# Splitting the experts' weights one expert ahead of the tiles that use them

## The reference, cut to what matters

```python
scores = x @ router_DE                       # 4096 rows, 8 experts
topv, topi = top_k(scores, 2)
gates = sigmoid(masked scores)               # 0 for experts not chosen
routed_in = x[None] * gates[:, :, None]
mid = einsum('ead,edf->eaf', routed_in, w_in_eDF)      # D 256 -> F 512
sw  = einsum('ead,edf->eaf', routed_in, w_swiglu_eDF)
h = silu(mid) * sw
out = sum over e of einsum('eaf,efd->ead', h, w_out_eFD)
```

## Time and profile before

| | |
|---|---|
| median of 3 runs | 1818.01 us (1816.95 to 1818.47) |
| profiled execution, its own time | 1816.74 us |
| its span | 1814.9 us |
| PE busy | 1610.9 us, 89% |
| DVE busy | 946.8 us, 52% |
| ACT busy | 958.7 us, 53% |
| POOL busy | 449.5 us, 25% |
| mean granted clock of PE | 0.945 |

### The profile page before, as it was taken

One profiled execution on the slowest core, in us unless ns is written; L12 is line 12 of the kernel. 1 busy time (PEld: TensorE's weight loads), 2 busy tenths in 40 slices (PEclk: granted clock), 3 DMA queues, 4 the chain that ended last, 5 costly groups with the idle time before them and its releaser, 6 DMA issues. The chain is left out here.

```text
span 1814.9 us, 30860 instructions
## 1 busy us (share of the span) xinstructions
PE 1610.9 (89%) x10249; PEld 1109.6 (61%) x10250; DVE 946.8 (52%) x1826; ACT 958.7 (53%) x1528; POOL 449.5 (25%) x496
## 2 busy tenths in 40 slices
PE   7859999999999948998569999999579976997998
PEld 5633333333333327887458888888468976896887
DVE  6523543635445447777743333333376555756784
ACT  5449999999999924444422222222133434333332
POOL 0001111111121112555522222222144003001664
PEclk9969999999999968999889999999789988998999
DMA  8982415514523047211411111111302010000001
GB/s 272 265 260 39 67 36 88 89 33 70 95 47 55 18 134 261 88 60 46 142 53 52 49 49 52 52 46 52 107 24 94 1 59 0 1 1 4 24 27 44
DMA packets 79455, 134.18 MB, mean 74 GB/s; under 512 B 11600, under 2 KB 45904, under 8 KB 76208
## 3 DMA queue, kind: packets, MB, share of 16 engines
q1 hardware_dynamic: 72360, 111.86, 23.9%
q0 software_dynamic: 6992, 20.95, 3.6%
HBM read 74.63 MB, written 58.14 MB: 73 GB/s over the span
## 5 line engine op out<-in xcount | busy, mean ns | idle before, releaser
L713 ACT ACTIVATE probs<-ps_s 128x1024 f32<-128x1024 f32 (+3 forms) x640 | 511.9, 941 | 10.5 <-PE ps_s L763 7.0
L780 PE MATMUL ps_o<-probs,V 128*17 128x512 f32 (+3 forms) x2560 | 292.6, 536 | 0.3 <-POOL probs L701 0.3
L701 POOL TENSOR_SCALAR_AFFINE_SELECT probs<-probs 128x512 f32<-128x512 f32 x128 | 83.3, 653 | 440.4 <-ACT probs L713 438.5
L1445 DVE COPY slot_hT<-ps_hT 128x512 f32<-128x512 f32 x71 | 49.1, 691 | 193.5 <-PE ps_hT L1488 193.5
L763 PEld LDWEIGHTS ps_s<-Q_even,K_even 50*128 50x128 f32 x640 | 55.7, 186 | 137.3 <-ACT probs L713 119.9
L1498 PE MATMUL ps_slot_y<-we_out,slot_hT 128*128 x568 | 134.6, 380 | 1.4 <-DVE slot_hT L1445 0.9
L763 PE MATMUL ps_s<-Q_even,K_even 50*128 50x512 f32 (+3 forms) x640 | 124.7, 445 | 12.0 <-DMA Q_even<-shift_parts 11.3
L1978 POOL TENSOR_TENSOR h_lo<-h,h_hi 128x512 fp32r<-128x512 f32 x64 | 89.5, 1416 | 182.4 <-DVE h L2024 182.4
L763 PEld LDWEIGHTS ps_s<-Q_odd,K_odd 50*128 50x128 f32 x640 | 55.1, 183 | 123.8 <-ACT probs L713 116.4
L763 PE MATMUL ps_s<-Q_odd,K_odd 50*128 50x512 f32 (+3 forms) x640 | 123.1, 439 | 0.4
L1403 POOL DMA_INDIRECT routed_rows<-slot_y,home_row x71 | 69.4, 977 | 178.5 <-ACT slot_y L1422 173.8
(11 more groups left out here) (280 smaller groups left out, 3969.9 us busy)
## 6 DMA issues: line engine op xcount, KB each, us to landing
qk_stacks<-qk_hi SPq DMA_DIRECT2D x64, 256.0 KB, 3.9
slot_rows<-slots_in SPq DMA_DIRECT2D x71, 128.5 KB, 2.0
qk_stacks<-qk_lo SPq DMA_DIRECT2D x32, 256.0 KB, 4.0
Q_odd<-qk_stacks SPq DMA_DIRECT2D x8, 768.0 KB
K_odd<-qk_stacks SPq DMA_DIRECT2D x8, 768.0 KB
Q_even<-qk_stacks SPq DMA_DIRECT2D x6, 768.0 KB
K_even<-qk_stacks SPq DMA_DIRECT2D x6, 768.0 KB
X<-x SPq DMA_DIRECT2D x8, 512.0 KB, 4.4
```

The source lines that it names most:

```text
L701: pool.affine_select(out=block_of, in_=block_of, compare_op=ALU.is_ge, fill=0.0, base=0, pattern=[[0, HG], [1, P]], channel_multiplier=-1) ...
L713: act.activation(probs[:, at % PROB_BUFS, 2 * p:2 * p + 2, off:BT], ps_s[:, s % SCORE_BUFS, :, off:BT], ACT.Exp).then_inc(exp_ok, 1)
L780: last = pe.matmul(ps_o[32 * h:32 * h + DH + 1, s % 2, off:BT], k["V"][:, group, SEQ_TILES * b + t, h, :], probs[:, at % PROB_BUFS, h, off ...
L1445: dve.tensor_copy(hT[:, :, :], ps_h[:, :, :]).then_inc(hT_ok, 1)
```

## The change: each expert's weights split during the tile before its first possible use

ACT, DVE and POOL split expert 0 ahead of the first tile, and expert i+1 at or near the end of their body i, for i from 0 to 6: ACT makes both high parts, DVE the low part of `we_in`, POOL that of `we_swiglu`. Each expert is given at least one tile, so that tile i never needs an expert beyond i. PE waits in tiles 0 to 7 for the low parts of expert i: before the first expansion for `in_low`, before the gated one for `gate_low` (in tile 0 both count in `in_low`). The third matrices are loaded in two halves of four, with the loads of the rows of tiles 2 and 3 between the halves and those of 4 and 5 behind. The first eight bodies are written out (`head=4`) in place of two.

```diff
-def over_blocks(eng, count, body):
+def over_blocks(eng, count, body, head=1):
     pairs = count // 2
-    for j in range(2):
-        body(j, j, 0)
-    if pairs > 2:
-        with eng.Fori(1, pairs - 1) as n:
+    for i in range(2 * head):
+        body(i, i % 2, i // 2)
+    if pairs > head + 1:
+        with eng.Fori(head, pairs - 1) as n:
...
-                    link(dve.tensor_scalar(padded[:, :], count[:, :], float(P - 1), None, ALU.add))
+                    link(dve.tensor_scalar(padded[:, :], count[:, :], float(P - 1), float(P), ALU.add, ALU.max))
...
-        w_in = sem(k, "experts_w_in")
+        outs_in = sems(k, "experts_out_in", "first_half second_half")
...
-        w_high, w_low, home_ok = sems(k, "experts", "w_high w_low home_ok")
-        halves = [(hi[:, e], lo[:, e]) for e in range(EXPERTS) for hi, lo in ((wi_hi, wi_lo), (wg_hi, wg_lo))]
-        def low_weights(eng, own):
-            for n, (hi, lo) in enumerate(halves):
-                if (n % 3 == 2) == own:
-                    eng.wait_ge(w_high, n + 1)
-                    eng.tensor_tensor(lo, lo.bitcast(F32), hi.bitcast(F32), ALU.subtract).then_inc(w_low, 1)
+        w_high, in_low, gate_low, home_ok = sems(k, "experts", "w_high in_low gate_low home_ok")
+        HALF_EXPERTS = EXPERTS // 2
+        def high_weights(act, e):
+            for hi, lo in ((wi_hi, wi_lo), (wg_hi, wg_lo)):
+                act.activation(hi[:, e], lo[:, e].bitcast(F32), ACT.Copy).then_inc(w_high, 1)
+        def low_weight(eng, hi, lo, e, m, done):
+            eng.wait_ge(w_high, 2 * e + m + 1)
+            eng.tensor_tensor(lo[:, e], lo[:, e].bitcast(F32), hi[:, e].bitcast(F32), ALU.subtract).then_inc(done, 1)
+        def splits_next(i):
+            return isinstance(i, int) and i + 1 < EXPERTS
...
 # SP
                 load(0, 0)
                 load(1, 1)
-                for e in range(EXPERTS):
-                    sp.dma_start(wo[:, e], ...).then_inc(w_in, 16)
-                with sp.Fori(0, SLOT_TILES // 2 - 1) as n:
+                for half in range(2):
+                    for e in range(HALF_EXPERTS * half, HALF_EXPERTS * (half + 1)):
+                        sp.dma_start(wo[:, e], ...).then_inc(outs_in[half], 16)
+                    for i in (2 * half + 2, 2 * half + 3):
+                        sp.wait_ge(home_ok, i - 1)
+                        sp.wait_ge(x_ok, i - 1)
+                        load(i, i % 2)
+                with sp.Fori(2, SLOT_TILES // 2 - 1) as n:
...
 # POOL, body i
-                low_weights(pool, True)
                 clear(pool, k["stale"])
...
                     if not is_last(i, SLOT_TILES):
                         find_home(i + 1, 1 - j, n + j)
+                    if splits_next(i):
+                        low_weight(pool, wg_hi, wg_lo, i + 1, 1, gate_low)
                     hold(pool, k, home_ok, i + 1)
                     hold(pool, k, y_ok, i + 1)
...
 # ACT, body i
                     if not is_first(i):
                         result(i - 1, 1 - j, n - (1 - j))
+                    if splits_next(i):
+                        high_weights(act, i + 1)
...
 # DVE, body i
                         x_rest(i + 1, 1 - j)
+                    if splits_next(i):
+                        low_weight(dve, wi_hi, wi_lo, i + 1, 0, in_low)
...
 # PE, body i
+                    if isinstance(i, int) and i < EXPERTS:
+                        pe.wait_ge(in_low, i + 2 if i else 1)
                     expand(i, j, e, ps_m, wi_hi, wi_lo, mid_ok)
                     if not is_first(i):
                         turn_h(i - 1, 1 - j)
+                    if is_first(i):
+                        pe.wait_ge(in_low, 2)
+                    elif isinstance(i, int) and i < EXPERTS:
+                        pe.wait_ge(gate_low, i)
                     expand(i, j, e, ps_g, wg_hi, wg_lo, gated_ok)
```

More of the change, by code:

```diff
@@ L1375, in _ @@
                 load(1, 1)
-                for e in range(EXPERTS):
-                    sp.dma_start(wo[:, e], io["w_out_e"][e].rearrange("(c p) f -> p c f", p=P)).then_inc(w_in, 16)
-                with sp.Fori(0, SLOT_TILES // 2 - 1) as n:
+                for half in range(2):
+                    for e in range(HALF_EXPERTS * half, HALF_EXPERTS * (half + 1)):
+                        sp.dma_start(wo[:, e], io["w_out_e"][e].rearrange("(c p) f -> p c f", p=P)
+                                     ).then_inc(outs_in[half], 16)
+                    for i in (2 * half + 2, 2 * half + 3):
[3 more added lines that the diff above has]
+                with sp.Fori(2, SLOT_TILES // 2 - 1) as n:
                     for j in range(2):
@@ L1406, in _ @@
                 find_home(0, 0, 0)
-                over_blocks(pool, SLOT_TILES, body)
+                over_blocks(pool, SLOT_TILES, body, HALF_EXPERTS)
                 for j in range(2):
@@ L1431, in body @@
                         result(i - 1, 1 - j, n - (1 - j))
+                    if splits_next(i):
+                        high_weights(act, i + 1)
                 act.wait_ge(k["experts_in"], 16 * 2 * EXPERTS)
-                for hi, lo in halves:
-                    act.activation(hi, lo.bitcast(F32), ACT.Copy).then_inc(w_high, 1)
+                high_weights(act, 0)
                 turned(0, 0)
-                over_blocks(act, SLOT_TILES, body)
+                over_blocks(act, SLOT_TILES, body, HALF_EXPERTS)
                 result(SLOT_TILES - 1, 0, SLOT_TILES // 2)
@@ L1458, in body @@
                         x_rest(i + 1, 1 - j)
-                low_weights(dve, False)
+                    if splits_next(i):
+                        low_weight(dve, wi_hi, wi_lo, i + 1, 0, in_low)
+                low_weight(dve, wi_hi, wi_lo, 0, 0, in_low)
+                low_weight(dve, wg_hi, wg_lo, 0, 1, in_low)
                 x_rest(0, 0)
-                over_blocks(dve, SLOT_TILES, body)
+                over_blocks(dve, SLOT_TILES, body, HALF_EXPERTS)
                 turned(SLOT_TILES - 1, 0)
@@ L1492, in contract @@
                     e = expert_of(i)
-                    if is_first(i):
-                        pe.wait_ge(w_in, 16 * EXPERTS)
+                    if isinstance(i, int) and i % HALF_EXPERTS == 0 and i < EXPERTS:
+                        pe.wait_ge(outs_in[i // HALF_EXPERTS], 16 * HALF_EXPERTS)
                     pe.wait_ge(hT_ok, i + 1)
@@ L1515, in _ @@
                 turn_x(0, 0, 0)
-                pe.wait_ge(w_low, len(halves))
-                over_blocks(pe, SLOT_TILES, body)
+                over_blocks(pe, SLOT_TILES, body, HALF_EXPERTS)
                 turn_h(SLOT_TILES - 1, 0)
```

## The result

The changed kernel takes 1832.68 us (median of 4 runs, 1830.9 to 1834.59), the kernel before 1817.48 beside it (4 runs, 1815.93 to 1818.47). The ratio is 1.0087, its 95% interval 1.0073 to 1.0101: slower by 15.2 us. The forecast was 1835.6, in a range of 1826 to 1849.

The account below looks back on a forecast made before the run. Weight splits bound the head of the experts' stage, PE its body (busy 10.00 of 10 us). Terms -17.7 + 32.8 + 2.5 = +17.6 on 1816.74 gave 1834.3, median 1835.6, range 1826 to 1849 us.

Parts of the forecast that it names:

- The head: Before the first tile: only expert 0 is split there, so PE starts 20.25 us earlier.
- Tile 1: Second tile: its gated expansion waits for POOL's split of expert 1, leaving the kernel 17.7 us ahead at the first contraction's end.
- The chain: Tiles 2 to 7: gated expansion waits for POOL's scatter, landing, home rows, low part; 5.46 us more each, 32.8 in all.
- The clock: Tiles 2 to 7: holes in PE's work lower its clock in some tiles; 2.5 us, ends 0 and 21.5.
- At nothing: Halved third matrices, cleared semaphores, maximum with 128 and written-out bodies cost nothing; bounds -1 and +3.
- The sum: Whole kernel: -17.7 + 32.8 + 2.5 = +17.6 us, median 1835.6.
- Only ACT and DVE bite: Rival, tiles 2 to 7: POOL's low part is on time; 3.24 us more each, sum +1.7, 1820 us; chance 0.06.
- The rival of hidden splits: Tiles 2 to 7: splits hide under PE's work if the second low part is ready by T + 1.6; 1800 us; chance 0.05.
- The rival of the lost clock: Half clock in nearly every one of tiles 2 to 7: 14 to 21.5 us instead of 2.5, 1850 us; chance 0.12.

Follow-up runs that it names:

- POOL first: Changed kernel with POOL's low part moved to the head of its body, before the wait for the scatter's landing: 1829.8 us, ratio 1.0047 to the kernel before.
- The shell alone: Changed kernel with the old splitting put back, all sixteen matrices before the first tile: 1823.0 us, ratio 1.0004 to the kernel before.
- filled, POOL first: Changed kernel with POOL's low part before the landing wait and ten unused matmuls filling PE's hole: 1825.8 us, ratio 1.0012 to the kernel before.
- two ahead: Changed kernel with body i splitting expert i+2 instead of i+1, at the same places in the bodies: 1808.2 us, ratio 0.9921 to the kernel before.

## Why the prediction was right

- *The head.* Told: PE starts 20.25 us earlier. Measured in the stage: 25.29 - 4.59 = 20.7.
- *Tile 1.* Told: 17.7 us ahead at the first contraction's end. Measured: 37.32 - 20.12 = 17.2. The low clock held PE in the first expansion (2.87 us of waiting, then a turning of 1.05), as the text had it as a possibility.
- *The chain.* Told: T + 10.65, 5.46 a tile, 32.8 in all. Measured: 10.23, 5.04 a tile, 30.2. The order and each wait are those of the forecast. PE's gated expansion came 0.52 us earlier in the tile than told, at T + 6.54. POOL's low part was 0.28 us shorter (2.34 instead of 2.62), and it started 0.23 us earlier (T + 4.07 instead of T + 4.30), since ACT's copy started at T + 0.03 instead of T + 0.13 and the scatter and the home rows followed. The 2.62 was misread as POOL's time alone. The row that shows it stands in the kernel before, just ahead of the 898.10 of the earlier trace rows:

```profile
897.29 1.22 DVE L1360 TENSOR_TENSOR we_swiglu<-we_swiglu,we_swiglu_hi 128x1024 fp32r<-128x1024 f32 x1
```

  This subtraction ended at 898.51, inside POOL's, and POOL's ended 2.21 us behind it. In the changed kernel's tiles 2 to 7 nothing of that kind ran on DVE when POOL started; the 2.39 of the earlier trace rows would have been the better row.
- *The clock.* Told: 2.5 us over the six tiles, because few of them would have the low clock behind the gated start. There it showed only as 3.68 us instead of 3.59, 0.5 in all. But it was low ahead of the gated start in every one of the six, not in some: the first expansion and the turning took 3.39 us in the tile shown, where 1.94 was told. Of the 2.22 us of waiting for POOL that I had counted as cover, the half clock ate 1.45 and POOL's being earlier 0.5; 0.28 were left, so the small price was a near thing. "POOL first" shows what it costs without the cover. A slip besides: by the rows PE works 5.2 of the 10.65 us, not 5.5.
- *At nothing.* The shell alone: 400.15 against 400.20. The two ends, -1 and +3, were wider than needed. In the faster pipelines the second half of the third matrices did probably cost something.
- *The sum.* Told +17.6; the stage gave -17.2 + 30.2 = +13.0, the medians +15.2. The other 2.2 us are in no row of the stage, so that the medians came so near to the forecast is in part luck.
- *The rivals.* "Only ACT and DVE bite" was told at 8.43 a tile and 1.7 us over before; the kernel in which this is so ("filled, POOL first") has 8.59 a tile and a stage 1.8 us over before's. It was the right price for another kernel. The rival of hidden splits named its point of decision: the splits must not stand behind the release of the result. In "two ahead" they still stand there, but are wanted a tile later, and the stage is 13.8 us under before's; with the orders changed and the third matrices spread it is 17.1. The rival of the lost clock was half there: every one of the six tiles ran in part at the half clock, but the clock was 0.83 in the windows, not 0.50, and the lost time lay beneath POOL's chain.

The Trainium skill's rule on the port pair of DVE and GpSimd ("SBUF — State Buffer", section "SBUF: two separate sides"), by which whoever is first keeps it for the whole instruction, agrees with the traces. POOL's low parts took 2.34 us when nothing of that kind ran on DVE. In "POOL first" the one at 935.70 started while DVE's low part was still running, took 2.45 and ended 2.23 us behind DVE's end at 935.92. The 2.62 of the earlier trace rows is of the same kind, so the prediction, which cited the rule for DVE's wait, had a case of POOL's wait in its own row.

## What to carry to other kernels

Work that fits by its amount can still be late: what is wanted for the next step has to be released by something before the end of this one. For each piece that is moved into a loop, follow its queue backwards to the last release that stands ahead of it; here that was a DMA's landing, on an engine (POOL) that was busy in 3.49 of 10 us. Where several waits end near the same point, the profile's list shows little of the one that counts: here it gave POOL 1.7 us in six tiles, though POOL set all of them. Only a kernel in which the others are taken away shows which one holds.

## What the runs showed of the hardware

A scatter issued by POOL took 1.00 us when it started 0.17 us before DVE's subtraction of two operands in SBUF (923.12 and 923.29 in the changed kernel), and neither was slowed. When it started inside that subtraction it took 1.80 (927.22 in "two ahead"), ending 0.88 behind DVE's end at 928.14, and DVE's own subtraction had taken 2.04 instead of 1.23, ending 1.08 behind the end of POOL's low part. Four scatters in "two ahead" did so, each ending 0.87 or 0.88 us behind DVE's end. The one scatter of 1.40 in the earlier trace rows, which I had set aside, ended 0.84 behind DVE's end at 880.37, so it was the sign of something regular.

In the changed kernel a hole of 2.87 us in PE's work came back every 10.2 us and the granted clock fell in each tile to the half for a part of it (0.83 in every window of 10 us from 910 to 970). With the hole filled down to 0.45 us it stayed at 1.00 from 910 us on.
